# The projection products of an attention step, in one burst or in two

## The reference, cut to what matters

```python
xn = layernorm(x)
q, k, v = (split_heads(xn @ W + b) for W, b in ((Wq, bq), (Wk, bk), (Wv, bv)))
probs = softmax(q @ k.T / sqrt(16))
ctx = merge_heads(probs @ v)
x = x + layernorm(ctx @ Wo + bo)
h = layernorm(x)
x = x + layernorm(quantized(silu(quantized(h, gate_w)) * quantized(h, up_w), down_w))
```

## Time and profile before

| | us |
|---|---|
| median of 3 runs | 1851.47 |
| lowest and highest | 1848.33, 1855.98 |
| profiled execution, its own time | 1853.87 |
| span of the profile | 1852.1 |
| TensorE busy | 1635.7 (88%) |
| VectorE busy | 1303.7 (70%) |
| ScalarE busy | 878.7 (47%) |
| GpSimd busy | 491.2 (27%) |
| mean granted TensorE clock | 0.938 |

### The profile page before, as it was taken

One profiled execution on the slowest core, in us unless ns is written; L12 is line 12 of the kernel. 1 busy time (PEld: TensorE's weight loads), 2 busy tenths in 40 slices (PEclk: granted clock), 3 DMA queues, 4 the chain that ended last, 5 costly groups with the idle time before them and its releaser, 6 DMA issues.

```text
span 1852.1 us, 28842 instructions
## 1 busy us (share of the span) xinstructions
PE 1635.7 (88%) x8328; PEld 767.2 (41%) x8328; DVE 1303.7 (70%) x2369; ACT 878.7 (47%) x1567; POOL 491.2 (27%) x384
## 2 busy tenths in 40 slices
PE   2599999999999999999999999854689999999996
PEld 1343343344344344344344343122355555555554
DVE  6279878878868868878878868789943443543444
ACT  2235755755755755755755755732222222222221
POOL 3012312312312312312222222355522222222222
PEclk9779999999999999999999999867899999999999
DMA  2302202201201201301211301333110110111020
GB/s 96 94 15 57 72 24 57 73 22 49 83 22 46 85 22 41 90 22 41 88 24 39 90 22 42 102 97 114 34 46 23 68 45 23 68 68 45 23 91 23
DMA packets 76479, 101.27 MB, mean 55 GB/s; under 512 B 15780, under 2 KB 40356, under 8 KB 76324
## 3 DMA queue, kind: packets, MB, share of 16 engines
q1 hardware_dynamic: 76328, 99.44, 18.1%
HBM read 51.65 MB, written 17.83 MB: 38 GB/s over the span
## 4 chain that ended last, share of the span: by engine, by line
PE 46%; issue 27%; DVE 18%; POOL 6%; ACT 2%; DVEq 0%; DMA 0%; SPq 0%; POOLq 0%; ACTq 0%
PE side L924 21%; PE contexts L988 10%; PE scores L976 7%; PE maxima_scores L961 5%; DVE maxima L778 5%; POOL fuse_low L1168 5%; DVE w_magic L131 1%; DVE y L737 1%; DVE qkT L764 1%; ACT probs L692 1%; DVE denominators L804 1%; DVE denominators L795 1%; DVE y L770 1%; DVE w_magic L133 1%; DVE ctx_raw L800 1%
## 5 line engine op out<-in xcount | busy, mean ns | idle before, releaser
L778 DVE TENSOR_REDUCE maxima<-maxima_scores 128x1 f32<-128x512 f32 x1024 | 655.7, 679 | 142.5 <-PE maxima_scores L961 128.3
L692 ACT ACTIVATE probs<-scores 128x512 f32<-128x512 f32 x1024 | 554.2, 597 | 379.9 <-PE scores L976 375.6
L961 PE MATMUL maxima_scores<-k_stack,q_stack 64*128 64x512 f16 x1024 | 334.9, 398 | 40.1 <-DVE maxima L778 39.7
L976 PE MATMUL scores<-q_stack,k_stack 64*128 64x512 f16 x1024 | 331.2, 396 | 14.3 <-ACT probs L692 7.0
L988 PE MATMUL contexts<-probs,v_one 128*32 128x512 f32 x2048 | 290.6, 641 | 12.5 <-DVE ctx_raw L800 8.6
L1267 DVE SCALAR_TENSOR_TENSOR fuse<-ring,up_scale,gate 128x512 f32<-128x512 f32 x96 | 71.9, 749 | 263.0 <-PE ring L1322 260.9
L539 POOL TENSOR_TENSOR denominators<-denominators,reciprocals 128x512 f32<-128x512 f32 x33 | 42.2, 1280 | 714.5 <-ACT reciprocals L655 714.5
L1168 POOL TENSOR_TENSOR fuse_low<-fuse,fuse_high 128x512 fp32r<-128x512 f32 x96 | 122.6, 1277 | 368.6 <-ACT fuse_high L1202 368.6
L976 PEld LDWEIGHTS scores<-q_stack,k_stack 64*128 64x128 f16 x1024 | 65.6, 95 | 334.5 <-ACT probs L692 215.1
L1337 PE MATMUL down_sums<-down_q,fuse_high 128*128 128x512 f32 x384 | 171.0, 445 | 30.1 <-POOL fuse_low L1168 30.1
L1322 PE MATMUL ring<-xT_high_ffn,gate_q 128*128 128x512 f16 x384 | 149.4, 389 | 7.0 <-DVE xT_low_ffn L1241 7.0
(11 more groups left out here) (151 smaller groups left out, 2429.7 us busy)
## 6 DMA issues: line engine op xcount, KB each, us to landing
q_stack<-qkT SPq DMA_DIRECT2D x192, 64.0 KB, 2.0
k_stack<-qkT SPq DMA_DIRECT2D x192, 64.0 KB, 2.0
x_rows<-in_L_attn_hidden_states SPq DMA_DIRECT2D x9, 1024.0 KB, 5.6
x_residual<-in_L_attn_hidden_states SPq DMA_DIRECT2D x36, 256.0 KB, 2.7
middle_rows<-y SPq DMA_DIRECT2D x36, 256.0 KB, 3.2
x_rows_ffn<-middle_rows SPq DMA_DIRECT2D x9, 1024.0 KB, 5.6
x_residual_ffn<-middle_rows SPq DMA_DIRECT2D x8, 1024.0 KB, 7.7
out_rows<-y_ffn SPq DMA_DIRECT2D x32, 256.0 KB, 2.2
```

The source lines that it names most:

```text
L692: act.activation(probs[:, n % 2, j, :], work[(GH * n + j) % RING][:], ACT.Exp, scale=float(D) ** -0.5).then_inc(p_full, 1)
L778: dve.tensor_reduce(maxima[:, g % 2, at:at + 1], bank[:], AX.X, ALU.max).then_inc(rot_free, 1)
L961: mm = pe.matmul(bank[:], q_st[half, s, qc * P:qc * P + P], k_st[half, s, :], start=True, stop=True)
L976: mm = pe.matmul(work[i % RING][:], k_st[half, s, c * P:c * P + P], q_st[half, s, :], start=True, stop=True)
```

## The change

The pieces lo to hi of a step were all issued at its end. Now the first half of them (rounded down) is issued in the middle of the step, behind the contexts of the step before and ahead of score 2, and the other half at the end. In step 0, which has no contexts ahead of it, the first half follows score 1 and its maximum product. A step with 12 products has 6 and 6, one with 6 has 3 and 3, one with 4 transposes 2 and 2. No instruction is added or taken away, and the other engines' programs stay as they are.

```diff
@@ -1024,9 +1024,12 @@
                         score(b, n, j)
                         if maxima_left:
                             share(j)
-                    if u == 0 and n:
-                        contexts(b, n - 1)
-                for c in range(lo, hi):
+                    if u == 0:
+                        if n:
+                            contexts(b, n - 1)
+                        for c in range(lo, (lo + hi) // 2):
+                            side_piece(later * SIDE + side_at[what, i], later, (what, i), c)
+                for c in range((lo + hi) // 2, hi):
                     side_piece(later * SIDE + side_at[what, i], later, (what, i), c)
                 share(GH if maxima_left else 0)
             contexts(b, STEPS - 1)
```

## The result

| | before | after |
|---|---|---|
| median, us | 1849.9 (4 runs, 1847.95 to 1855.98) | 1903.24 (4 runs, 1900.19 to 1906.89) |
| profiled execution, us | 1853.87 | 1900.19 |
| span, us | 1852.1 | 1898.4 |
| mean granted TensorE clock | 0.938 | 0.961 |

The ratio is 1.0283, 95% interval 1.0252 to 1.0315. The change makes the kernel slower by 2.8%; 1912 was forecast, within 1866 to 1940. The two profiled executions differ by 46.3 us. Ahead of the first step the program is the same, yet the changed execution gets there 4.7 us earlier (107.6 us against 112.3), at a granted clock of 0.91 where it had been 0.67 (80 to 100 us). From the first score of the pass to the last it takes 50.6 us more.

What follows compares the result with a forecast made beforehand. Product steps were taken as bound by TensorE, the others by VectorE, besides the loop's edge. Terms sum to 8.2 us a batch, 3.8 in the last, 61 in all: 1912 us forecast, range 1866 to 1940.

Steps and rivals of the forecast that it cites:

- (A): In 19 product steps of a batch, entering and leaving a second burst costs 0.19 us each, 3.6 us a batch.
- (B): Behind the contexts TensorE waits for bank `side`, 0.33 or 0.25 us in product steps; with transposes 4.1 us a batch.
- (C): In steps 2, 6 and 30 VectorE first copies transposed maxima, delaying products by 0.29 us more each, 0.9 a batch.
- (D): In steps 5, 13, 21 and 29 ScalarE's late reads make VectorE begin 0.26 us later, 1.0 us a batch.
- (E): In step 0 three of v's six products move ahead of the 2.34 us wait, a gain of 1.43 us.
- rival 3: In step 0 TensorE returns from the pause at full clock, gaining 4.8 us a batch; 1841 with waits hidden; 7%.
- Rival 1: The waits behind the contexts do not show, only the second burst's cost and step 0's gain; 1868 us; 13%.
- Rival 2: Pauses in product steps make the granted clock fall twice more a batch, 27 us on top, 1939 us; 13%.
- Rival 4: No measurable change, within 0.5%: the 9.4 us a batch in which TensorE isn't busy swallow the delays; 7%.

Runs made afterwards that it cites:

- e8: Kernel before with the change's split in all steps but step 31; 1903.98 us, ratio 1.0285.
- e9: Changed kernel with VectorE's read of the products' bank ahead of its first maximum of the step; 1895.46 us, ratio 1.0206 to the kernel before.
- e2: Kernel before with two bursts a step, the first behind score 2 and its maximum; 1882.51 us, ratio 1.0170.
- e1: Kernel before with only the wait for the bank moved behind the contexts, all products in one burst at the end; 1901.53 us, ratio 1.0276.
- e3: Kernel before with only step 0 of a batch split; 1829.85 us, ratio 0.9894.
- e4: Kernel before with all steps but step 0 split; 1918.87 us, ratio 1.0367.
- e6: Kernel before with only the four steps with transposes of x split; 1853.17 us against 1852.82, ratio 1.0003.
- e11: Kernel before with three extra, thrown-away products behind score 1 of step 0, the burst of six staying at its end; 1830.98 us, ratio 0.9874.
- e12: Kernel before with step 0's whole burst behind score 1, and the last q item's products moved from steps 10 and 11 to 9 and 10; 1821.54 us, ratio 0.9823.
- e5: Kernel before with step 0's whole burst of six products behind score 1, none at its end; 1829.08 us, ratio 0.9873.

## Why the prediction was right, and where it wasn't

**What bounds the kernel.** Right outside the loop's edge: the product steps 4 to 8 grew by what TensorE lost in them, and steps 22 to 24, in which nothing moved, grew by nothing. At the edge step 31 grew by 1.80 us where the terms have 0.52, and step 0 got that back, since VectorE sets the pace there (e8).

**(A), the second burst.** Right, 0.19 forecast and 0.21 measured in the steps of six products where nothing waits (11, 19 and 27: 3.87 against 3.66; 26: 4.57 against 4.36), 0.16 to 0.19 in steps 6 to 8 of e9, where the wait is taken away. In step 3 it didn't show: 3.87 against 3.90, for that step was 0.24 longer than its like already before. That products follow contexts by 1.00 as scores do was an assumption and holds (e9). The rule of the Trainium skill that I weighed ("TensorEngine Tiling (Array Packing)", "Key Properties": a change of mode drains the array) would have given half of that, one more change a step. The steps show the whole 0.19 or more. By the same count e2 makes two changes of mode more than the kernel before, and costs 0.30; so the cost grew with the count, but not at one price each (0.21 for one, 0.30 for two), and the count alone does not give the cost here.

**(B), the wait.** Right in mechanism and size: 0.33 and 0.27 (products at 1.86 and 1.80, not 1.53). e9 has the burst without the wait, and in steps 7 and 8 it takes back 0.27 of the change's 0.46 and 0.45. e1 has the wait without the burst; its price there is higher, 0.52 in step 4 (0.41 until score 2 goes out, and 0.11 by which the pair behind the wait starts apart). So the two runs show both costs, but they don't add up to the change's 0.56.

**(C) and (D).** Right where the working can be followed: step 6 takes 5.97 where the terms give 2.24 + 1.59 + 0.53 + 1.59 = 5.95, and step 5 takes 5.87 for 5.83. (D) in steps 13 and 21, which VectorE bounds, was 0.1 and not 0.26. Step 2 missed by more: it grew by 1.23 us where the terms give 0.81. Its contexts start at 1.16 and not at 0.53, because the second maximum product waits for VectorE, and its products at 2.61; that wait was not in the sum. Step 12 grew by 0.80 for 0.52; why is open.

**Steps 14 to 18.** The sum is close (0.53 against 0.36) by luck. Steps 14, 15, 16 and 18 grew by 2.3 us together, six times what I gave them, and step 17 became 1.77 shorter without its fall of the clock, which the prediction did not have.

**(E), the gain in step 0.** This is the term that was mis-sized: "so 1.43 leaves the path" (three of six products at the lower clock). Measured alone it is 3.50 us a batch (e3; e4 and the change differ by 3.3 at the edge), since the clock falls behind the pause at one passage of seven and no longer at all of them. It is the mechanism of rival 3, which I held for possible and put at 4.8. That 4.8 counts something twice: the stretch of 6.8 us at 0.50 has the six products in it, so half of it already brings them back to 1.43, and three of them leaving are then worth some 0.8 more and not 1.43. By my own rows rival 3 comes to about 4.2, by the runs to 2.8 and 0.7. What I had against it was the sum of the costs, and that did hold. I should have taken it into the forecast's range from both sides instead of leaving it to a rival. With 3.5 for 1.43 in each of the eight batches the sum of 61 us comes to 44.5, or 1898.4 for the profiled execution; it took 1900.2. That they agree to 1.8 us is luck in part. The pass itself grew by 50.6 us and the start gave 4.7 back; and the first batch, whose step 0 has no loop's edge ahead of it, saved 1.1 us in steps 0 and 1, not 3.5.

**The rivals.** Rival 1 (waits hidden) fell by the rows of steps 4 and 7. Rival 2 (the clock falls more often in product steps) fell as well: granted 1.00 over steps 2 to 8 with pauses of 0.2 to 0.64 us in six of the seven. Its premise, that the product steps ran at 1.00 without a break, was not exact: the clock fell in step 10, behind the waits of step 9, in all eight batches of the kernel before. Rival 3 was right in its mechanism and wrong in its outcome: the gain of 3.5 stayed below the cost of the other steps. Rival 4 (pauses swallow the delay) fell with the steps' own lengths.

**Open.** Which pauses make the clock fall and which don't was not found out. Of the seven passages from one batch to the next, the traces show 0.50 at all seven in the kernel before, e1 and e4 and at six in e6, none of which sends products ahead of the pause in step 0; at one in the change, e3 and e11, and at none in e12, which do. But e5, e8, e2 and e9 do so too, and have it at three, four, six and six. So products ahead of the pause went with a clock that stays in most kernels and are not enough by themselves. The falls behind step 9 and in step 17 came and went between kernels whose steps there are the same (e5 and e11 against e3). All totals carry this uncertainty, those of e2, e8, e9 and e12 above all, so they are read by steps.

## What to carry to other kernels

When work moves forward on an engine's queue, look at what its first instruction waits for, and compare that with the new place: here a bank that is free at 1.86 us of a step cost nothing at 2.07 and 0.33 us at 1.53, in a dozen steps of each batch. Interrupting a dense burst has a price by itself (0.2 to 0.3 us here). And what paid here was filling a pause that exists anyway: splitting only the step with such a pause gave 1.1%, splitting all steps lost 2.8%.

## What the runs showed of the hardware that I had not expected

Three products that nobody uses, placed ahead of a pause on TensorE, made the kernel 1.3% faster (e11: 1830.98 against 1854.12 us), mostly because the granted clock behind the pause stayed at 1.00, 2.4 GHz, at six of seven passages, where it had been at 0.50, 1.2 GHz, over 6.8 us. What TensorE did before: in the kernel before it paused for 0.91 us, sent seven small matmuls, and paused for 2.34; in e11 it paused for 1.19 and 1.35 with ten between. Pauses of 0.2 to 0.64 us in the product steps 2 to 8 of the changed kernel did not cost the clock. It is no rule, though: in e2 and e9, which also have three products ahead of that pause, the clock fell at six of seven passages.

After a pause on TensorE a score and the maximum that goes with it start 0.11 us apart where they otherwise start together (e1), so a wait of 0.41 cost the step 0.52.
